# A graph network's adjacency build: ScalarE's loop over units turned by half a unit, its table load in mid-unit, the last unit written out, and the branch for unsorted edges placed ahead of the loop

## What is computed

```python
def _spmm(src, dst, w, x, n):
    return jax.ops.segment_sum(w[:, None] * x[src], dst, num_segments=n)
...
for W, b, g, be in ((W1, b1, g1, be1), (W2, b2, g2, be2)):
    agg = _spmm(src, dst, edge_weight, x, n)
    h = (x + agg) @ W + b
...
out = jax.ops.segment_sum(msg, dst, num_segments=n_nodes)   # in gcn_conv
```

## Time and profile before

| | us |
|---|---|
| median of 3 runs | 2048.79 (2047.58 to 2049.47) |
| the profiled execution, its own time | 2048.91 |
| its span | 2047.0 |
| mean granted TensorE clock | 0.949 |
| PE busy | 1791.3 (88%) |
| DVE busy | 930.7 (45%) |
| ACT busy | 605.9 (30%) |

### The profile page before, as it was taken

One profiled execution on the slowest core, in us unless ns is written; L12 is line 12 of the kernel. 1 busy time (PEld: TensorE's weight loads), 2 busy tenths in 40 slices (PEclk: granted clock), 3 DMA queues, 4 the chain that ended last, 5 costly groups with the idle time before them and its releaser, 6 DMA issues.

```text
span 2047.0 us, 31184 instructions
## 1 busy us (share of the span) xinstructions
PE 1791.3 (88%) x10360; PEld 1412.7 (69%) x10364; DVE 930.7 (45%) x1708; ACT 605.9 (30%) x1076; POOL 149.8 (7%) x163
## 2 busy tenths in 40 slices
PE   2588988888777799999999999979999999998992
PEld 1288888777676577777777777756667777676871
DVE  5899999788777101111103323332220332235343
ACT  0023567777777410000001111233320000004540
POOL 2000000000000000000000000000000000140354
PEclk8789999899898789999999999989999999999996
DMA  2041133333334854444444343400017434433554
GB/s 86 21 142 80 80 160 160 160 160 160 160 160 195 277 152 137 136 143 144 148 142 128 112 128 114 127 1 0 0 49 247 120 119 125 133 120 117 163 156 138
DMA packets 108624, 260.96 MB, mean 127 GB/s; under 512 B 13005, under 2 KB 65383, under 8 KB 103067
## 3 DMA queue, kind: packets, MB, share of 16 engines
q1 hardware_dynamic: 90874, 240.29, 34.4%
q0 software_dynamic: 5568, 12.82, 2.0%
q10 hardware_dynamic: 12128, 7.16, 1.5%
HBM read 160.44 MB, written 108.04 MB: 131 GB/s over the span
## 4 chain that ended last, share of the span: by engine, by line
issue 53%; PE 29%; ACT 7%; DVE 6%; ACTq 3%; POOL 1%; DMA 1%; DVEq 1%; SPq 0%; POOLq 0%
PE ps L1732 11%; PE ps L1798 5%; PE ps L1733 4%; ACT ps L711 3%; ACT wide L705 3%; PE ps L1993 2%; PE ps L2009 2%; ACTq L696 2%; DVE act_c L1195 1%; PE ps L1704 1%; PE ps L1815 1%; POOL act_c L1016 1%; PE ps L2001 1%; PE ps L1985 1%; DMA act_c<-expert_replies,pair_tab 1%
## 5 line engine op out<-in xcount | busy, mean ns | idle before, releaser
L1732 PE MATMUL ps<-early,act_c 128*128 128x200 bf16 x3600 | 473.0, 261 | 102.9 <-ACT ps L679 57.2
L1798 PE MATMUL ps<-wide 128*128 128x320 f32 (+1 forms) x2000 | 534.8, 428 | 2.9 <-DVE pair_tab L1435 2.9
L1798 PEld LDWEIGHTS ps<-wide 128*128 128x128 f32 x2000 | 379.3, 191 | 145.2 <-DVE pair_tab L1435 3.0
L1732 PEld LDWEIGHTS ps<-early,act_c 128*128 128x128 bf16 x3600 | 343.0, 101 | 135.4 <-issue 127.5
L1733 PE MATMUL ps<-early,act_c 128*128 128x208 bf16 x1200 | 316.6, 264 | 0.0
L1798 PE MATMUL ps<-wide,act_a 128*128 128x320 f32 (+1 forms) x1000 | 268.3, 431 | 8.8 <-ACTq L744 8.8
L1195 DVE TENSOR_TENSOR act_c<-act_c,pair_tab 128x3072 bf16<-128x3072 bf16 x150 | 262.3, 1749 | 0.0
L1798 PEld LDWEIGHTS ps<-wide,act_a 128*128 128x128 f32 x1000 | 192.0, 192 | 82.6 <-issue 11.8
L705 ACT COPY wide<-ps 128x816 f32<-128x816 f32 x200 | 167.1, 836 | 174.5 <-PE ps L1733 135.3
L1299 DVE TENSOR_TENSOR wide<-ps,rows 128x1280 f32<-128x1280 f32 x10 | 14.9, 1492 | 409.1 <-PE ps L1815 409.1
L711 ACT ACTIVATE ps<-ones 128x816 f32<-128x816 f32 x200 | 170.6, 853 | 8.1
(11 more groups left out here) (232 smaller groups left out, 1498.3 us busy)
## 6 DMA issues: line engine op xcount, KB each, us to landing
wide<-weight_matrix SPq DMA_DIRECT2D x90, 800.0 KB, 4.5
weight_matrix<-wide SPq DMA_DIRECT2D x20, 2000.0 KB, 6.2
count_matrix<-wide SPq DMA_DIRECT2D x20, 2000.0 KB, 10.8
wide<-count_matrix SPq DMA_DIRECT2D x45, 800.0 KB, 4.5
expert_replies<-wide SPq DMA_DIRECT2D x63, 128.0 KB, 1.9
wide<-weight_matrix SPq DMA_DIRECT2D x20, 400.0 KB, 3.7
rows<-routed_tokens SPq DMA_DIRECT2D x42, 128.0 KB, 2.3
wide<-count_matrix SPq DMA_DIRECT2D x10, 400.0 KB, 3.9
```

Of the source, the lines that this page charges most:

```text
L1732: nc.tensor.matmul(weights, hot_lane[:, slot, part, two, :, k], hot_key[:, slot, two, 0:WCOLS, k], start=False, stop=True, skip_group_chec ...
L1798: i = nc.tensor.matmul(ps[:, 2 * sub + h, 0:n], features[:, q * QUADS + t, h * P:(h + 1) * P], moving, start=q == 0 and t == 0, stop=q == ...
```

## The change

The order of ScalarE's work inside a group is kept, and so are the groups' order and the semaphores that others wait for. Four things change.

- **The turn.** The loop now begins in the middle of a unit: it does the second five groups of a unit, the degrees row, then `stage_free` and the first five groups of the next unit. The first half of the first unit stands ahead of the loop.
- **The table.** Its rows are shifted by five groups, so that one row of ten values serves the second half of one unit and the first half of the next. There are 21 rows for 20, of which the first and the last are loaded with five values. VectorE writes it with four instructions for three.
- **The end.** The loop runs four times for five; the last four units are written out behind it. In the last unit the groups 6 to 9 are only copied, without zeros and self loops, since nobody uses their banks again.
- **The branch.** The block for unsorted edges now stands ahead of the block with the loop.

```diff
-            with act.If(disordered < 1):
-                ...
-                with act.Fori(0, SUPERS) as s:
-                    for u4 in range(4):
-                        half = u4 % 2
-                        stage_free(s * 2 + u4 // 2, half)
-                        _, ends = nc.values_load_multi_w_load_instructions(
-                            end_tab[:, ds(s * (4 * ENDS) + u4 * ENDS, UGROUPS)], ...
-                        for k in range(UGROUPS):
-                            ...
             with act.If(disordered > 0):
                 act.wait_ge(tables_ready, 1)
...
+            with act.If(disordered < 1):
+                for b in range(SETS):
+                    act.activation(ps[:, b * GROUP:(b + 1) * GROUP, 0:PCOLS], zero, ACT.Copy, scale=0.0)
+                act.drain()
+                for b in range(SETS):
+                    self_loops(b * GROUP, b, 0).then_inc(acc_free, 1)
...
+                def take_group(s, u4, k, end, again):
+                    half, group = u4 % 2, u4 * UGROUPS + k
+                    first_bank = group % SETS * GROUP
+                    group_ps = ps[:, first_bank:first_bank + GROUP, 0:PCOLS]
+
+                    act.wait_ge(pair_done, end)
+                    act.copy(stage[half][:, :, k * GCOLS:(k + 1) * GCOLS].rearrange("p r (b j) -> p b r j", b=GROUP),
+                             group_ps.rearrange("p b (r j) -> p b r j", j=WIN)).then_inc(copies_done, 1)
+
+                    act.wait_ge(copies_done, s * (4 * UGROUPS) + group + 1)
+                    if k == UGROUPS - 1:
+                        act.sem_inc(unit_complete, 1)
+                    if again:
+                        act.activation(group_ps, zero, ACT.Copy, scale=0.0)
+                        act.drain()
+                        self_loops(first_bank, group + SETS, s).then_inc(acc_free, 1)
+
+                def units_of(s, last):
+                    for u4 in range(4):
+                        final = last and u4 == 3
+                        ends = ends_at(s * 4 + u4 + 1, HALF if final else UGROUPS)
+                        for k in range(HALF, UGROUPS):
+                            take_group(s, u4, k, ends[k - HALF], not final or k < UGROUPS - SETS)
+                        degrees_of(u4, u4 % 2, s).then_inc(unit_summed, 1)
+                        if not final:
+                            following = (u4 + 1) % 4
+                            s_of = s + 1 if u4 == 3 else s
+                            stage_free(s_of * 2 + following // 2, following % 2)
+                            for k in range(HALF):
+                                take_group(s_of, following, k, ends[HALF + k], True)
+
+                ends = ends_at(0, HALF)
+                stage_free(0, 0)
+                for k in range(HALF):
+                    take_group(0, 0, k, ends[k], True)
+                with act.Fori(0, SUPERS - 1) as s:
+                    units_of(s, False)
+                units_of(SUPERS - 1, True)
             compute_end(act, 1)
```

48 lines of the change are left out of this document (18 added, 30 removed).

## The result

The changed kernel takes 2040.17 us (median of 7 runs, 2038.5 to 2043.92) against 2048.79 (7 runs, 2047.58 to 2050.03): 8.6 us less, ratio 0.9956, 95% interval 0.9945 to 0.9967. The forecast was 2028. The profiled execution took 2038.5 us, its span is 2036.6. It is the fastest of its seven, while the profiled execution of before stands at its median; so the pair of profiles differs by 10.4 us where the medians differ by 8.6.

The account below looks back on a forecast made before the run. VectorE was taken to bound the build before about 400 us, ScalarE from there. Turn -19, end -7.1, clock -1 and start +6.5 sum to -20.6 from 2048.9: 2028 us, range 2016 to 2041.

Parts of the forecast that it names:

- three quarters of the 24: Ten build units from 424.3 to 661.7 us: of ScalarE's 24 us shed, 18 us reach the end.
- the 19 forecast: Whole gain of the turn in the build, -19 us, with bounds of 0 and -28.
- VectorE's floor of 207 us: Ten build units: 180 us of VectorE's work plus boundary stalls of 2.7 us each, near ScalarE's floor of 213.
- a sign of being wrong: Named beforehand for the build: VectorE's boundary stalls staying at 4 to 6 us would show the forecast wrong.
- second rival: Build: TensorE's long loads and lower clock hold VectorE, only 10 of 19 us come through, 2037 us; chance 0.13.
- the writes make the load long, not its values: ScalarE's table loads at unit ends: moved past the writes, 19 loads of 3.44 us become about 1.0 us.
- The end, -7.1: Last copy to TensorE's first product: the 6.13 us gap behind the branch goes, 7.9 us become 0.8.
- The start, +6.5: Moved branch at 102.7 us: ScalarE's code fetch delays the build by 6.13 us plus a little, from 0 to 24-25.
- The first rival: Start of the build: the code fetch waits behind the fill, 17 or 24 us, giving 2039 or 2046; chance 0.15.
- The clock at the first product, -1: After the build: with a shorter gap TensorE may stay at 2.4 GHz, gaining 1 us, at most 1.9.
- Everything behind the build hangs on `compute_done` and shifts with it.: Stretch after the build: it was to move with the build's end, adding 0 us of its own.
- The fourth rival: ScalarE's loop: the longer body no longer fits, one 6.1 us fetch per unit, 2078 us, slower; chance 0.05.

Follow-up runs that it names:

- small_writes_high32: Changed kernel with 32-bit masks, 18 of 20 units writing only partitions 112 to 127; 2022.1 us, ratio 0.9867, 24 us under its control.
- ctl_before: Kernel before with TensorE's accumulator wait value masked to eight bits and ScalarE's table of ends holding 16-bit numbers; 2137.17 us, ratio 1.0413.
- turn_by_two16: ctl_after with its loop turned by two groups and not by five, so ScalarE's load stands beside the write-out; one run, 2113.09 us.
- branch_only: ctl_before with only ScalarE's branch for unsorted edges moved ahead of the loop, loop not turned; 2133.54 us, ratio 1.0393.
- fill_first32: Changed kernel with 32-bit masks, HBM-to-HBM fill issued before the stage's end and not behind it; 2071.15 us, ratio 0.9951.
- turn_only32: Changed kernel with 32-bit masks, block for unsorted edges put back behind the loop; 2083.34 us, ratio 1.0007.
- turn_only: ctl_after with the block for unsorted edges put back behind the loop; 2057.13 us, ratio 1.005.
- loads_late32: Changed kernel with 32-bit masks, last 19 of ScalarE's 33 weight DMAs issued behind the diagonals; 2083.92 us, ratio 1.0007.
- fill_first32_again: The kernel of fill_first32 run once more, beside ctl32_after_third; 2043.38 us, ratio 0.9973, 2.5 us under the control.
- ctl_after: Changed kernel with TensorE's accumulator wait value masked to eight bits and ScalarE's table of ends holding 16-bit numbers; 2061.2 us, ratio 1.005.
- delay32: ctl32_after_third with eight more zero fills of ScalarE, each with a drain, ahead of the signal that ends the build; 2060.7 us, ratio 1.0038.
- ctl32_after_third: Changed kernel with 32-bit table, ScalarE's ten values per unit and TensorE's wait value masked, third run of this control; 2045.86 us, ratio 0.9986.
- 32-bit controls: Changed kernel with 32-bit table and masks on ScalarE's and TensorE's wait values, run three times; ratios 0.9988, 0.9984 and 0.9986.
- masked base: Changed kernel with 32-bit table and masked wait values on ScalarE and TensorE, on which later experiments stand; ratios 0.9988, 0.9984 and 0.9986.
- the first group: The runs of fill_first32 beside its control, the changed kernel with 32-bit masks; 2071.15 us against 2079.31.

## Why the prediction was wrong where it was

**"From the ten units ScalarE sheds 24 ... I take three quarters of the 24, 18 us."** The mechanism was right and the size was not. The loads shrank by 2.4 us as forecast, ScalarE's issue time by 24.0 of 24. But 11.1 us came through in those ten units for 18, and 14.7 in the build for the 19 forecast. The term that failed is VectorE's floor of 207 us, and with it the three quarters. I set it with boundary stalls of 2.7 us taken from the units before 424 us, and held TensorE's loads at what they were. In the stretch after, VectorE stalls 44.0 us in ten units, 4.4 each, which I had named as a sign of being wrong; and TensorE's loads in them grew by 13.1 us in sum, as 12 of 27 now ran beside a write-out for 8. This is my second rival, "VectorE and TensorE take over", to which I gave 0.13, at about half of its price (10 of 19 us come through). That TensorE's loads are what holds VectorE there is argued from their sum and from TensorE's "issue" (10.3 to 25.1 us); small_writes_high32 fits it with 12.4 us, and does not isolate it. A cost that was raised in a test was no guide to what comes back when it is lowered: 0.76 us per microsecond of longer load (ctl_before), 14.7 us for 46 (0.32) of shorter.

**"So the writes make the load long, not its values."** Half right. The writes do, and turn_by_two16 settles it. But the values matter too: 16-bit numbers more than double every load at either place, and five values take 0.55 us where ten take 0.99.

**The end, -7.1.** Measured -7.2. The 6.13 us went with the jump over the block, and branch_only removes them alone (7.95 to 1.99 us).

**The start, +6.5.** The stall was 5.7 us (ScalarE's first instruction behind it at 108.80 us, where before it followed the branch of 102.7 us at once), and 5.0 at the first copy. "Its price is that of the only such branch in the trace" held. What it depends on is now known: 2.4 us with all but empty queues (fill_first32 twice, turn_only32's back-branch), 2.5 and 2.8 right behind `unit_complete` (the ends of turn_only and turn_only32), 5.4 to 8.9 beside the HBM-to-HBM fill, 6.1 and 6.9 beside a write-out. That it waits for traffic is shown by fill_first32, where only the fill was moved; that it waits for code is read from the fetch on queue 14 that lies in each of these gaps. The first rival, a fetch of 17 or 24 us, did not occur.

**The clock at the first product, -1.** The clock term held: TensorE did start at 2.4 GHz, and up to `dinv_row`'s copy it was busy 1.63 us less, with 10.2 us at half clock for 14.1. What I had put at nothing is the wait behind it: TensorE now reaches the diagonals before ScalarE has them and waits 2.44 us, so that the stretch came out at +0.8. The copy of the degrees, from which the diagonals come, stood behind ScalarE's DMA issues ("issue", 40.10 us). loads_late32 freed it and gained nothing, but against a control without that wait; whether the issues cost after its 2.44 us stays open.

**"Everything behind the build hangs on `compute_done` and shifts with it."** This is the step that failed worst, 5.6 of the 10.2 us by which the pair of profiles missed. What the runs showed in its place: the build's end came 16.8 us earlier at the first product and only 10.4 at the end, and all of the 5.6 us lies in stretches where the granted clock differs, none where it is equal. Behind `dinv_row`'s copy TensorE stood at half clock for 56.8 us before and for 70.0 after. The other traces say the same. Here are the ten kernels that ran where the kernel before takes about 2049 us (before, fill_first32_again, small_writes_high32, after, ctl_after, delay32, ctl32_after_third, branch_only, ctl_before, turn_only), with the stretch from `dinv_row`'s copy to the end, which none of them changed but small_writes_high32, in what it reads:

```
half-clock us in it   56.8    62.9    69.7    70.0    73.3    73.5    73.7    79.2    79.3    87.5
the stretch, us       1291.6  1294.1  1297.1  1297.2  1299.1  1298.8  1299.1  1303.9  1304.1  1305.9
```

That is 0.47 us for each microsecond at half clock, whatever the shift. (On the chip where the kernel before takes 2081 us and more, the same stretch took 1324 us with 87 at half clock up to 1341 with 119.) delay32 shows that a shift can also pass unchanged. What sets the half-clock time of an execution is not shown: the changed kernel's 7 runs spread over 5.4 us and those of before over 2.5, and its 32-bit controls over 14. So how much of the 5.6 us is a lasting cost of the change, and how much the draw of one execution, stays open. By the medians 12.0 of the 20.6 us forecast are missing, 1.8 more than by the profiles, mostly because the profiled execution of after was its fastest (1.7 us under its median); no trace shows where they lie.

**The fourth rival, "the loop no longer fits"**, did not happen in this change. It happened in two experiments that added 40 instructions to a pass. The price beside a write-out was near the 6.13 us that I took, 6.9, and 2.4 in mid-unit, but once per pass and not per unit.

**A version better than both** can't be shown outright, since the controls, which are compared with, stand some 0.3% above the changed kernel. On the masked base, fill_first32 beat its control by 0.33% and 0.13% and the kernel before by 0.49% and 0.27%. Only in the first group do the two intervals over the kernel before (0.9931 to 0.9971 and 0.9967 to 1.0001) all but part. Issuing the fill ahead of the stage's end is the one step that the runs recommend; how it does on the change as it stands wasn't tried.

## What to carry to other kernels

When the bound engine is relieved, ask what stands next with the very same cause: here the other engine's table loads in the same write-out, which had to be read from the trace and not taken from stretches where they did not yet bind, and which fell beside the write-outs more often once the first cause was gone. Where TensorE's clock moves between its two levels, a time gained ahead is not simply carried to the end: compare windows of equal program content and their granted clock before you look for a new wait, and use medians for anything under 10 us. And a taken branch over a long block should be put where the DMA queues are empty: with that alone the jump took 2.4 us for 8.3.

## What the runs showed of the hardware that was not expected

- A register load of ten 16-bit values took 2.13 to 2.16 us, of ten 32-bit values 0.99 to 1.03; beside the write-out 8.6 and 3.4.
- A load is slowed even by a write-out of an eighth of the bytes (16 partitions), and at least as much at its start: a TensorE load that starts 0.8 us behind the unit's end took 4.9 us beside partitions 112 to 127 and 5.5 beside 0 to 15, for 3.6 to 4.1 beside the full write-out. So it is not the bytes alone; what else, the runs do not show.
- A loop pass of 296 records of ScalarE paused at each back-branch (6.9 us), one of 299 in another layout did not, and the same 299 elsewhere in the program paused again (2.4 us). The kernel with the 6.9 us pauses has 43 fetches on queue 14, the one without pauses 23. A jump with such a fetch took 2.4 us past all but empty queues. The Trainium skill ("Runtime: NRT & Kernel Launch", Instruction fetch mechanics) says that a taken branch out of the fetched window waits for a DMA fetch; the traces agree, and add that the wait beside other traffic was 2.2 to 3.7 times as long (5.4 to 8.9 us for 2.4).
- The same build code, in two kernels on one chip (ctl32_after_third and delay32, one profiled execution each), differed by 13 us, with 34 us more at half clock on TensorE in the longer one.
